# A recommender tower on one Trainium2 core: a block's diagonal products in one row, and x's turning moved to the fourth tile

## The reference

```python
x0 = xk = e
for W in (W0, W1):                                  # W0: 39*39 x 128, W1: 39*128 x 128
    Wr = W.reshape(39, xk.shape[1], 128)
    xk = einsum('bid,bjd,ijh->bhd', x0, xk, Wr)     # x1, then x2
    outs.append(xk)
z = concatenate(outs, axis=1).sum(axis=-1)          # (512, 256)
h = concatenate([z, dense_ctx], axis=1)             # (512, 272)
h = relu(h @ W_top1 + b_top1)                       # 512
h = relu(h @ W_top2 + b_top2)                       # 256
y = h @ W_top3                                      # (512, 1)
```

## Time and profile before

| what | value |
|---|---|
| three runs | 377.39, 377.59, 378.48 us, median 377.59 |
| profiled execution, first to last instruction (span) | 376.0 us |
| median of the runs less that span | 1.6 us |
| TensorE busy | 227.8 us (61%) |
| VectorE, ScalarE busy | 159.5 and 156.7 us (42% each) |
| GpSimd busy | 110.4 us, all of it before 148 us |
| granted TensorE clock | 1.00 in every stretch |

### The profile page before, as it was taken

The page is one execution under the profiler, slowest core; times in us unless marked ns, Lnnn a source line. Parts: engine busy times, 40 slices in busy tenths (PEclk is TensorE's granted clock), DMA queues, the critical chain, the costliest instruction groups (busy, mean ns, idle before and its releaser), DMA issues.

```text
span 376.0 us, 4521 instructions
## 1 busy us (share of the span) xinstructions
PE 227.8 (61%) x1601; PEld 173.6 (46%) x1601; DVE 159.5 (42%) x313; ACT 156.7 (42%) x302; POOL 110.4 (29%) x119
## 2 busy tenths in 40 slices
PE   4311101001000010168999899998999999999997
PEld 4200000000000000055667588766778877788897
DVE  4350000000100000037989676897775767756411
ACT  4600000000200000027789766797786677865511
POOL 5777777777777775000000000000000000000000
PEclk9999999999999999999999999999999999999999
DMA  6800000000000000000921000000000000000000
GB/s 177 239 12 9 7 7 6 7 6 7 6 7 6 7 6 6 0 0 3 260 86 40 0 3 2 1 2 0 3 1 2 0 2 2 2 2 0 2 0 2
DMA packets 8218, 8.71 MB, mean 23 GB/s; under 512 B 2951, under 2 KB 5804, under 8 KB 8196
## 3 DMA queue, kind: packets, MB, share of 16 engines
q1 hardware_dynamic: 4516, 7.48, 7.0%
q0 software_dynamic: 3680, 0.95, 2.7%
HBM read 8.42 MB, written 0.00 MB: 22 GB/s over the span
## 4 chain that ended last, share of the span: by engine, by line
PE 50%; issue 36%; ACT 6%; DVE 4%; another core or an unknown queue 2%; DMA 1%; ACTq 0%; DVEq 0%
PE turn_bank L524 10%; PE pair_bank L445 5%; PE x_bank L469 5%; PE g_bank L502 5%; PE x_bank L471 4%; PE x_bank L472 4%; DVE onehot L771 2%; ACT prod_hi L1006 2%; PE g_bank L686 2%; PE x_bank L481 2%; PE turn_bank L562 2%; ACT prod L1001 2%; PE turn_bank L535 1%; PE x_bank L695 1%
## 5 line engine op out<-in xcount | busy, mean ns | idle before, releaser
L420 POOL DMA_INDIRECT emb<-tbl,ids_sb x115 | 110.2, 958 | 37.2 <-issue 34.7
L1001 ACT ACTIVATE prod<-pair_bank 128x512 f32<-128x512 f32 (+1 forms) x112 | 65.8, 599 | 40.8 <-PE pair_bank L445 36.0
L843 DVE TENSOR_TENSOR prod_lo<-prod,prod_hi 128x512 fp32r<-128x512 f32 x96 | 64.8, 685 | 2.7
L469 PE MATMUL x_bank<-prod_hi,pair_w_hi 128*128 128x512 f32 (+1 forms) x112 | 63.1, 564 | 1.8 <-DVE prod_lo L843 1.3
L445 PE MATMUL pair_bank<-x,sel 117*128 117x512 bf16 (+1 forms) x112 | 42.8, 384 | 0.9 <-ACT x L983 0.7
L524 PE MATMUL turn_bank<-g_sb,w_sb 128*128 128x128 f32 x312 | 42.2, 278 | 0.0
L524 PEld LDWEIGHTS turn_bank<-g_sb,w_sb 128*128 128x128 f32 x312 | 39.4, 191 | 3.1 <-issue 1.4
L686 PE MATMUL g_bank<-tab_parts,onehot 125*128 125x96 bf16 x36 | 7.4, 251 | 54.5 <-issue 54.5
L1006 ACT ACTIVATE prod_hi<-prod 128x512 fp32r<-128x512 f32 x64 | 40.1, 626 | 0.1
L471 PE MATMUL x_bank<-prod_lo,pair_w_hi 128*128 128x512 f32 x96 | 37.8, 394 | 0.0
L472 PE MATMUL x_bank<-prod_hi,pair_w_lo 128*128 128x512 f32 x96 | 37.7, 392 | 0.0
(11 more groups left out here) (140 smaller groups left out, 333.4 us busy)
## 6 DMA issues: line engine op xcount, KB each, us to landing
emb<-tbl,ids_sb POOLq DMA_INDIRECT x115
tab<-small SPq DMA_DIRECT2D x2, 560.0 KB
wt<-w_top SPq DMA_DIRECT2D x2, 512.0 KB, 4.5
tab<-small SPq DMA_DIRECT2D x1, 504.0 KB
wa<-pair_w_a SPq DMA_DIRECT2D x1, 448.0 KB
wb<-pair_w_b SPq DMA_DIRECT2D x1, 448.0 KB
wtd<-w_dense SPq DMA_DIRECT2D x1, 256.0 KB
dense_sb<-dense_t SPq DMA_DIRECT2D x1, 256.0 KB
```

The lines of the kernel that those rows point to most:

```text
L420: pool.indirect_dma_start(out=emb[:, at:at + D], out_offset=None, in_=tables[f], in_offset=bass.IndirectOffsetOnAxis(ap=ids_sb[:, c * M + ...
L469: mm = pe.matmul(x1_banks[k % 2][:, :], pair_w_hi[p, t, :], hi(n), start=(t == 0), stop=(t == FULL))
L843: dve.tensor_tensor(lo(n), prod[rows, n % RING, :], prod_hi[rows, n % RING2, :], ALU.subtract).then_inc(lo_done, 1)
L1001: act.activation(prod[0:ROWS[t], n % RING, :], pair_bank[n % 2][0:ROWS[t], :], ACT.Square).then_inc(sq_done, 1)
```

## The change

- `contract_d`: both pairs of a block stand in one row, in the step where layer 1 is at tile 4 (t1 of the block after next). Pair 1 goes into misc_bank (columns 160 to 480, behind the turned x) and into the block's own x1 bank, so it doesn't wait for pair 0's copies. Both engines copy both pairs at t2.
- `turn_x` moves from t0 to t3, `spread_x` from t2 to t4. `turn_x(k)` now also waits until ScalarE has copied the G of block k - 2, since they share misc_bank; layer 1's first tile of a block waits until VectorE has copied the G that lay in its x1 bank.
- The later lookups: the twenty products of a part stand in one step (t4), in the two G banks; the one-hots are made earlier. In chunk 0 they fall into blocks 0 and 1, in chunk 1 into blocks 5 and 6. The same sixteen fields are looked up, and the same 115 rows of gathers are left.
- In `seam()` both pairs of block 2 stand behind layer 1 of tile 25 (before: pair 0 behind tile 24, pair 1 behind tile 27).

The diff, cut to its core (the lookups' bookkeeping of semaphore values is left out):

```diff
-G_AT = (3, 6)
+G_AT = 4
+G_KEPT = 2
+XT_AT = 3
+SPREAD_AT = 4
...
-LOOKED = (3, 1, 1, 0)
+PARTS = (0, 2, 2, 0)
+LOOK_AT = 4
...
+        def look_step(c, part):
+            return ((c - 1) * NB + part + (c > 1)) * NT + LOOK_AT
+        def hot_at(n):
+            return [(c, part, r) for c in range(1, NCH) for part in range(PARTS[c]) for r in range(HOT)
+                    if max(look_step(c, part) - 6 + r, 0) == n]
...
             if k == K - 1 and pair == 1:
                 return (turned_x1(k) if half else misc_bank)[:, 0:2 * QC]
+            if pair == 1 and not ended(k):
+                return x1_banks[k % 2][:, 0:2 * QC] if half else misc_bank[:, QC:3 * QC]
             return g_bank[half][:, 0:2 * QC]
...
             def turn_x(k):
                 wait(pe, xblk_done, k)
                 pe.wait_ge(x3_b, k // NB + 1)
+                wait(pe, g_act, 2 * (k - 1))
...
             def layer1(n):
                 if t == 0:
                     wait(pe, x1_done, k - 1)
+                    wait(pe, g_dve, 2 * (k - 1))
-                    c, j = divmod(k, NB)
-                    if j in (1, 2) and c + 1 < NCH and LOOKED[c + 1]:
-                        pe.wait_ge(picked, picks(c + 1, j - 1))
...
             def turn_x1(k):
                 pe.wait_ge(x1_kept, k + 1)
+                if k == K - 1:
+                    pe.wait_ge(g_dve, 2 * k)
...
             def contract_d(k, pair):
                 if pair == 0:
                     pe.wait_ge(x1_done, k + 1)
-                    pe.wait_ge(xblk_done, k + 1)
-                if k == K - 1 and pair == 1:
+                    pe.wait_ge(xblk_done, k + 1 if ended(k) else min(k + 2, K))
+                    pe.wait_ge(picked, len(SETS) + looks_ahead_of((k + 2) * NT))
+                    wait(pe, g_act, 2 * k)
+                    wait(pe, g_dve, 2 * k)
+                elif k == K - 1:
                     pe.wait_ge(x1_done, K + 1)
-                else:
-                    wait(pe, g_act, 2 * k + pair)
-                    wait(pe, g_dve, 2 * k + pair)
+                elif ended(k):
+                    pe.wait_ge(g_act, 2 * k + 1)
+                    pe.wait_ge(g_dve, 2 * k + 1)
...
             def seam(c):
                 for m in range(n - LAG1, n):
                     layer1(m)
-                    if m % NT in G_AT:
-                        contract_d(k - 2, G_AT.index(m % NT))
+                    if m % NT == G_AT:
+                        contract_d(k - 2, 0)
+                        contract_d(k - 2, 1)
...
             # TensorE's step
-                if t == 0 and n < TILES:
+                if t == XT_AT and n < TILES:
                     turn_x(n // NT)
                 if u == 0 and k >= 1 and not ended(k - 1):
                     turn_x1(k - 1)
-                if u in G_AT and k >= 1 and not ended(k - 1):
-                    contract_d(k - 1, G_AT.index(u))
+                if u == G_AT and k >= 1 and not ended(k - 1):
+                    contract_d(k - 1, 0)
+                    contract_d(k - 1, 1)
...
-                if c + 1 < NCH and LOOKED[c + 1]:
-                    if j in (0, 1) and t == NT - 1:
-                        wait(pe, x1_done, n // NT)
-                        look_up_later(c + 1, j, 0, 2)
-                    if j in (1, 2) and t < 2:
-                        look_up_later(c + 1, j - 1, 2 * t + 2, min(2 * t + 4, HOT))
+                for part in look_at(n):
+                    look_up_later(*part)
...
             # VectorE's step (ScalarE's keep_g likewise)
-                if t == 2:
-                    spread_x(k)
-                if t == 1 and k >= 2 and not ended(k - 1) and not ended(k - 2):
+                if t == G_KEPT and k >= 2 and not ended(k - 1) and not ended(k - 2):
                     keep_g(k - 2, 0)
+                    keep_g(k - 2, 1)
-                if t == 4 and k >= 2 and not ended(k - 1) and not ended(k - 2):
-                    keep_g(k - 2, 1)
+                if t == SPREAD_AT:
+                    spread_x(k)
```

More of the change, by code:

```diff
@@ L77 @@
 NS = 25
-LOOKED = (3, 1, 1, 0)
+PARTS = (0, 2, 2, 0)
+LOOK_AT = 4
+SLOTS = LATER * sum(PARTS)
+HEAD_SLOTS = 16
 PIECES = ((0, 16), (16, NS), (NS, M))
@@ L320, in lookups @@
         def lookups(c):
-            return sum(LOOKED[:c + 1])
+            return len(SETS) + sum(parts > 0 for parts in PARTS[:c + 1])
         def gathers(c):
@@ L431, in turn @@
                 pe.wait_ge(split_done, pieces(c))
+                kept = 2 * (c * NB - (1 if c in SEAMS else 2))
+                if c and part == 0:
+                    pe.wait_ge(g_dve, kept)
+                if c and part == 1:
+                    pe.wait_ge(g_act, kept)
                 d0, d1 = TURNS[part]
@@ L504, in contract_d, with look_up_later, spread_later @@
                 mm.then_inc(g_mm, 1)
[L506 to L510, removed]
+            def look_up_later(c, part):
+                pe.wait_ge(picked, len(SETS) + nth(c, part))
+                pe.wait_ge(dense_dve, 2)
+                wait(pe, g_act, 2 * (look_step(c, part) // NT - 1))
+                wait(pe, g_dve, 2 * (look_step(c, part) // NT - 1))
+                for r in range(HOT):
+                    pe.wait_ge(later_hot_done, HOT * nth(c, part) + r + 1)
                     for f in range(LATER):
[L512 to L515, removed]
+                        rows = tab_parts[part // 2][:, LATER * (part % 2) + f, 2 * r:2 * r + 2, :, :]
+                        mm = pe.matmul(later_cols(f), later_hot[:, r, f, :],
+                                       rows.rearrange("p r q d -> p (r q d)"), start=(r == 0 and f % 2 == 0),
+                                       stop=(r == HOT - 1 and f % 2 == 1))
                     mm.then_inc(later_row, 1)
+            def spread_later(q, bank):
+                for s in range(8 * q, min(8 * q + 8, SLOTS)):
+                    c = [s < LATER * sum(PARTS[:n + 1]) for n in range(NCH)].index(True)
+                    f = s - LATER * sum(PARTS[:c])
+                    mm = pe.transpose(halved(bank)[:, s % 8 * CH:(s % 8 + 1) * CH],
+                                      half_h[:, c, f:f + 1].to_broadcast([128, SP]), eye_h[:, :])
+                mm.then_inc(later_spread, 1)
             def layer2(c, i0, i1):
@@ L665, in _ @@
                 if f == 7:
[L667 to L671, removed]
+                    for q in range(HEAD_SLOTS // 8):
+                        spread_later(q, later_id_bank[q])
             for n in range(len(SETS)):
@@ L794, in pick_later @@
                 dve.wait_ge(looked_ok, picks(c, part))
[L795 to L798, removed]
-            def words(n, c=0):
[L802 to L806, removed]
+                for half in range(2):
+                    f0 = LATER * part + 2 * half
+                    last = dve.copy_predicated(later_looked[:, f0:f0 + 2, :, :].rearrange("b f q d -> b f (q d)"),
+                                               odd[:, c, f0:f0 + 2].unsqueeze(2).to_broadcast([128, 2, E]),
+                                               later_rows(half, 1))
+                last.then_inc(picked, 1)
+            def words(n, c=0):
+                f0, w = (0, LATER * PARTS[c]) if c else SETS[n][:2]
+                done = lookups(c) if c else n + 1
+                dve.wait_ge(picked, picks(c, PARTS[c] - 1) if c else n + 1)
+                low, words_in = (later_low[:, 0:w * D], later_looked[:, 0:w, :, :]) if c else (
+                    low_word[:, f0 * D:(f0 + w) * D], looked[:, f0:f0 + w, :, :])
                 dve.scalar_tensor_tensor(low.rearrange("b (f d) -> b f d", d=D), words_in[:, :, 2, :], 256.0,
@@ L1057, in step @@
                         keep_g(k - 1, 1)
-                if t == 2 and looks and j in (1, 2):
-                    keep_looked_later(c + 1, j - 1)
+                for part in look_at(n - 1):
+                    keep_looked_later(*part)
                 tile(n)
@@ L1115, in keep_looked_later @@
             def keep_looked_later(c, part):
[L1116 to L1127 removed]
+                act.wait_ge(later_row, HOT * (nth(c, part) + 1))
+                for half in range(2):
+                    f0 = LATER * part + 2 * half
+                    last = act.activation(later_looked[:, f0:f0 + 2, :, :].rearrange("b f q d -> b f (q d)"),
+                                          later_rows(half, 0), ACT.Copy)
+                last.then_inc(looked_ok, 1)
+            for q in range(HEAD_SLOTS // 8):
+                keep_later_ids(q, later_id_bank[q])
             keep_table(0)
```

66 lines of the change are left out of this document (34 added, 32 removed).

## The result

The changed kernel takes 380.03 us (379.90 to 382.10, 4 runs), the kernel before on the same chip 377.49 (376.73 to 378.48, 4 runs): a ratio of 1.0079, interval 1.0051 to 1.0108, slower by 2.5 us. The forecast was 380.5.

A forecast was written before the change was run, and what follows sets the result against it. TensorE was taken to bound the tile steps from 174 us on, with ScalarE's copies newly exposed at t3 and t4 (68%). Block terms summed to +2.9 us: 377.6+2.9 = 380.5 us, range 377.5 to 383.0.

The forecast's parts named there:

- Light block: Blocks without layer-2 products: row saves 0.30, waits at x's turning (0.33) and x1's (0.45) lose about 0.75; +0.44 us each.
- Start: Blocks 0 and 1, bound by VectorE: block 2's first select at 189.1 for 189.55, 0.53 less lookup; -0.95 us, bounds 0 to -3.0.
- Block 3 and the first chunk change: Block 3: VectorE's chain before the chunk change 0.5 us later; seam: both G rows after tile 25 delay x1h, +0.9.
- Blocks 8 and 12: No layer 1 at t3, so turning x1 waits 0.83 us for x1h; with the row's saving, +0.6 each.
- Blocks 9 and 13: The last MLP product (0.53 us) stands between the two waits and covers the second; +0.1 each.
- Heavy blocks: Blocks 10, 11, 14, 15: merging saves row entries and weight reloads, x's turning before L524 gives back 0.23; -0.17 us each.
- 0.27 to its start: Heavy blocks: x's turning before L524 takes 0.27 us to L524's start, against 0.10 for the turning alone.
- The end: After tile 111's layer 1: turning waits 0.87 us instead of 1.07, but the whole 1.38 row stands before; +0.3.
- Rival 1: Faster: the G row hides nothing, so only the savings remain; -4.0 us, 373.6 us; chance 8%.
- Rival 2: No change: light blocks' waits half as long and the start gains 2 us; about 377.9 us; chance 15%.
- Rival 3: Much slower: layer 1 of t0 waits for VectorE's G copies, at TensorE's t4; 0.5 more in eight blocks, 384.5 us; 6%.
- Rival 4: The head, slow for an unnamed reason, moves as code behind it changes; 1 to 5 us either way; chance 3%.

The follow-up runs named there:

- n_double: Changed kernel without the gathers of chunks 1 to 3, ScalarE's copy of the second pair made twice: 244.12 us, beside 241.86 without the extra copy.
- n_fix: Changed kernel without chunks 1 to 3's gathers; x turned later, x1h before the rounding outside splitting blocks; first chunk change and end reordered: 239.25 us, beside 241.86.
- n_seam: Changed kernel without chunks 1 to 3's gathers; at the first chunk change, G row behind tile 27's layer 1, x1h before G copies: 241.27 us, beside 241.86.
- fix_full: Changed kernel with all gathers and the four moves of n_fix: 377.96 us, ratio 1.0005 to the kernel before.
- pick_full: fix_full without the later turning of x in blocks 0, 1, 4, 8, 12 and without x1h first in block 1: 377.47 us, ratio 0.9996 to before.

## Why the prediction was right

The forecast (+2.9, ScalarE's copies exposed at t3 and t4) came true in the sum, in the place and in the cause; n_double and n_fix show the cause from both sides. How close the sum came (+3.2 in the steps) is partly luck: its terms erred by 1.2 us in all one way and by 0.9 the other. The terms, at equal work (twelve lookup products are 0.53, twenty 0.86, so stages with them are not compared bare):

- **Light block, +0.44; measured +0.57** (8.22 before, by the prediction's rows, and 8.79 after in block 2; before's block 2 took 8.72, 0.53 of it lookups). Every event was placed to about 0.1: the second copy done at 4.95 after t0's select, the turning seen at 5.06; x1h done at 6.44, x1 turned at 6.46. Mis-sized were the signal from ScalarE's copy to the turning, 0.15 and not 0.05, and the turning of x1 behind idle time: 0.50 to the next select and not 0.43.
- **Start, -0.95; measured about -0.65** (-0.13 at block 2's first select, -0.53 of lookups). Inside the bounds.
- **Block 3 and the first chunk change, +0.5 and +0.9; measured +0.59 and +0.75.** n_seam gives 0.64 of the latter back: it was the row of sixteen ahead of layer 1 of tiles 26 and 27, as forecast. VectorE's share in block 7 is as forecast too: the low part of tile 53 starts 9.81 us after the block's first select instead of 9.26.
- **Blocks 4 to 6, +0.54; measured +0.39.** Block 7, +0.5; measured +0.53.
- **Blocks 8 and 12, +0.6 each; measured +0.74.** The wait for x1h was forecast at 0.83 and is there; the idle time before the turning is 0.68 in block 8. The copies have no part in it: they are done at 263.44, and ScalarE then waits for t3's select.

```profile
263.00 0.44 ACT L1081 ACTIVATE g_sb<-misc_bank 128x320 f32<-128x320 f32 x1
264.19 0.60 ACT L1051 ACTIVATE prod<-pair_bank 128x512 f32<-128x512 f32 x1 [0.75 <-PE pair_bank L482]
```

- **Blocks 9 and 13, +0.1 each; measured +0.22.** The MLP product covers the second wait, as forecast; none of the eight waits is theirs.
- **Heavy blocks, -0.17 each; measured -0.32.** The step that failed: "0.27 to its start". That row stands right behind a chunk change and does not carry over. In block 11 the first layer-2 product starts 0.12 behind the start of x's turning, and the six take 0.75 where six without it take 0.66 (297.24 to 297.90). So moving the turning gave back 0.11 (0.12 less 0.10, and 0.09) and not 0.23:

```profile
298.36 0.27 PE L491 MATMUL misc_bank<-sel,x 117*128 117x39 bf16 x4
298.48 0.91 PE L578 MATMUL turn_bank<-g_sb,w_sb 128*128 128x128 f32 x6
299.23 0.38 PE L482 MATMUL pair_bank<-x,sel 117*128 117x512 bf16 x1
```

- **The end, +0.3; measured +0.4.** Here too the wait for x1h is the reason, in the changed kernel:

```profile
357.03 0.40 PE L505 MATMUL x_bank<-prod_hi,pair_w_hi 96*128 96x512 f32 x1
357.91 0.60 PE L519 MATMUL x_bank<-idf,x1h 128*128 128x128 f32 x3 [0.47 <-ACT x1h L1071]
```

**Copies or missing row.** No run separates how much of a light block's loss is the two copies' and how much the missing second row's. An estimate from the rows of block 7: with no copies ahead of it, t3's square would start 0.42 after its select, at 250.29 and not 250.50, and x1's turning at 251.96 and not 252.17. Then 0.2 of the 0.8 us of waiting are the copies'; the other 0.6 would stand as one wait for x1h, since no G row lies between t3's select and that turning any more. n_double shows that a longer copy is paid in full, not that the copies are the whole price.

**The rivals.** Rival 1 needed light blocks of 7.9 us; they are 8.8. Rival 2 needed waits half as long; they are 0.44 and 0.38 for 0.33 and 0.45. Rival 3's wait, layer 1 of a block for VectorE's copies, appears in none of the light blocks. Rival 4 is undecided: the head was 0.9 shorter in the profiled execution, but the first select lies between 173.1 and 174.2 us in the profiles of four kernels (before, after, fix_full, pick_full) whose heads are alike. The steps alone would have made +3.2; the medians differ by 2.5. The prediction's own bounds have a slip: with the seam's 0 as well as the start's -3.0 the low end is 377.6 and not 378.4; the result lies inside either.

The drain rule that was weighed (the Trainium skill, TensorEngine Tiling (Array Packing), Key Properties) has its price here, and the trace agrees with its sign: in block 10 two rows with their entries and exits cost 0.4 more than one. In the light blocks that gain was lost, and more, in waits for copies out of PSUM. The page's PSUM Bottleneck section says that this copying may become the limit once TensorE is faster; here it did so by its place in ScalarE's order, not by its sum (ScalarE is busy 32.4 of 43.5 us in the second chunk).

## What to carry to other kernels

Merging two short rows on the engine that binds saves their entry and exit (0.3 to 0.4 us here), but first ask what the second row was hiding: here it covered the making of x1h, and its loss, together with the copies' being made at once, cost more than the merge saved. When copies are gathered into one place, what is queued behind them on the copying engine moves by their whole sum, so reorder that engine's queue in the same edit; a short experiment is to double one copy and see whether the step grows by its duration. And a move that is right in one kind of block is not so in blocks with other work: x1h ahead of the rounding helps where VectorE has time to spare and hurts where it splits, since VectorE waits for that rounding. Test two moves apart before blaming one of them.

## What was not expected of the hardware

- **The head depends on the chip, and the later gathers.** With all gathers the steps began at 26 us on one chip and at 173 to 174 us in every other profile. On chips of the second kind, leaving out the gathers of chunks 1 to 3 and the waits for them brought it to 34.2 to 35.6. Which of a gather's traits slows TensorE's lookups so was not tried.
- **Half the clock cost the head nothing.** In runs of one kernel (before, 17 runs beside fix_full) spans were 374.8 to 377.6 us at a mean granted clock near 0.79 and 375.5 to 376.6 at 1.00. The head is bound by something else than TensorE's speed. One run of the changed kernel, at 0.996, took 382.1 for 379.9 to 380.1; that stays unexplained.
- **In the steps the clock does cost.** After 1.59 us of idle time the granted clock was 0.50 for the 2.4 us shown, and sixteen products took 2.4 us (70.61 to 73.04) that take 1.3 at 1.00.
